# Second attention: score units of two PSUM banks, with separate banks for plain and turned scores

## The chip, the cores and the metric

One of the eight cores of a Trainium2 chip runs the program. A core has TensorE (PE: matrix products into PSUM, with PEld its weight loads), VectorE (DVE), ScalarE (ACT), GpSimd (POOL) and SyncE (SP, which issues the DMAs); each has its own queue, worked in order, and they meet at semaphores only. PSUM has 8 banks of 128 x 512 float32, and every matmul writes into one of them. The metric is the device time of one execution in microseconds, the median of several runs.

## The reference, cut to what matters

Six layers with residuals run over 8 sequences of 256 tokens with 128 channels: a mixture of experts, a linear attention with four blocks, the first mixture again, a mixture with expert choice (top-k), a causal attention with 16 heads of width 8, and the expert-choice mixture again. The change is in the causal attention:

```python
qkv = x @ W_attn + b_attn                 # x: layer-normed, [8, 256, 128]
q, k = rope(q), rope(k)                   # angles by head index; 16 heads, width 8
att = einsum('bhqd,bhkd->bhqk', q, k) / sqrt(8)
att = softmax(where(causal, att, -inf), axis=-1)
y = einsum('bhqk,bhkd->bhqd', att, v)
return y @ W_proj + b_proj
```

## The kernel before, in words

All semaphores and the order on every engine are written out by hand. The stage `attn1` has a function on each engine. A block `tb` is 512 tokens, two sequences. Per block, `project_in` (PE, 8 projections of 3 matmuls each) makes rotated queries and keys, which ScalarE (`hm`, L1475) and VectorE (`stk`, L2026) add and split into the stacked operand `stk`; `hm` has two buffers, so it may run at most two ahead of `stk`. In `stk` a head has 32 rows, so that a score product uses 32 of PE's 128 rows; four heads `g` with the same head group `hg` lie in the four row groups.

Each sequence's scores are computed twice. The **plain** scores (queries by keys, L955, with the causal mask added by further matmuls, L964 and L969) serve only for the row maximum, which VectorE takes from PSUM (L2034). The negated maxima are turned by PE (`maxima`), copied by ScalarE to `mT` (L1480), and put by a DMA into spare rows of `stk` (semaphore `m_placed`). The **turned** scores (keys by queries, L955 too) then come out with the maximum already subtracted; ScalarE takes the exponential from PSUM (`exps`, L1485), POOL zeroes the upper triangle (L2212), and PE multiplies by the values with a column of ones (`outputs`, L997 and L1000). ScalarE copies that to `ot` (L1490), PE flips it (L1008), VectorE divides (`normalise`, L2007 and L2010). Per block the result is turned (`turn`), split (yoT high on ScalarE, `low` on VectorE), projected (`project_out`) and added to the residual (`add`, L2019). The values of a block go through `values` (PE), vT (ScalarE), `values_turned` (PE) and a copy into `vaug` (VectorE).

Plain and turned scores of a sequence each have three units: `k` = 0 is the first half of the plain queries (16 products of 128 columns; for turned, `k` = 2), the others are 8 products of 256 columns, two head groups each. A unit fills four banks, one for each `g`, and one maximum or one exponential reads all four (128x2048). Banks 0 to 3 hold plain 0, plain 2, turned 0 and turned 1 in turn; banks 4 to 7 hold plain 1 and turned 2, and 4 and 5 also the outputs, 6 and 7 the flip, the values, the turning and the projections.

The loop (L1035) has ten passes, s = -1 to 8. A pass takes the plain scores of sequence s+1, the turned scores of s and the outputs of s-1, and its order on PE is: turned 0, plain 1, plain 0, (values or two projections), outputs of two head groups, plain 2, (two projections), the other outputs, turned 1, maxima, flip, turned 2, (four projections). "First" passes (s even) stack the next block if there is one, half of it between the maxima and half at the end of the pass; "second" passes (s odd) take the next block's values and the last block's output projection. With s = 7 the first parts of the following layer's norm and of its router start (`ln_centre`, `ln_variance` L573, `scores` L589), which lead to the top-k on VectorE.

Of the kernel before, what the change touches and what calls it, by code (L numbers as in the profile page):

```python
# [14 lines left out]
P = 128  # L15
# [17 lines left out]
HG = 4  # L33
# [103 lines left out]
def macaron(nc, a, const, out):  # L137
# [3 lines left out]
    with es:  # L141
# [169 lines left out]
        EARLY_BANK, LATE_BANK = {LN_FFN1: 4, LN_FFN1B: 6}, 2  # L311
# [25 lines left out]
        OUT_BANK, TURN_BANK = 7, (7, 7, 7, 6)  # L337
        V_BANK = 6

        def stack_bank(tb, k):  # L340

            if tb == 0:
                return k
            if tb == 1:
                return (4 if k < HG else 6) + k % 2
            return 6 + k % 2 if k < HG else k - HG

        def stack_mid(tb):

            return HG if tb == 1 else 0  # L350
# [179 lines left out]
        def _(pe):  # L530
# [405 lines left out]
            def attn1():  # L936
# [22 lines left out]
                def plain(s, k):  # L959

                    if k == 0:
                        products(0, s, 0, 1, 0, 0, P, range(HG), False)
                        for g in range(4):
                            ins = pe.matmul(ps[:, g, :], ident_b[:], cmask[:], start=False, stop=True, skip_group_check=True)  # L964
                    else:
                        bank = 4 if k == 1 else 0
                        products(bank, s, 0, 1, P, 0, SEQ, (2 * k - 2, 2 * k - 1), False)
                        for g in range(4):
# [4 lines left out]
                def turned(s, k):  # L973

                    if k < 2:
                        ins = products(0, s, 1, 0, 0, 0, SEQ, (2 * k, 2 * k + 1), True)
                    else:
                        ins = products(4, s, 1, 0, P, P, P, range(HG), True)
                    ins.then_inc(t_ready, 1)

                def maxima(s):
                    pe.wait_ge(mneg_done, s + 1)
                    for q in range(2):
                        ins = pe.transpose(ps[0:2 * HEADS, 6, q * P:(q + 1) * P],
# [41 lines left out]
                def project_out(tb):  # L1026
                    pe.wait_ge(yol_done, tb + 1)
                    mm3(pe, ps[:, OUT_BANK, :], wvp_hi[:, 1, :], wvp_lo[:, 1, :], yoT_hi[:], yoT_lo[:]).then_inc(proj_ready, 1)
# [6 lines left out]
                for s in range(-1, SEQS + 1):  # L1035
# [3 lines left out]
                    if 0 <= s < SEQS:  # L1039
                        if second and more and tb > 0:  # L1040
                            pe.wait_ge(stk_done, (tb + 2) * 2 * HG)
                        elif s > 0:
                            pe.wait_ge(exp_done, 3 * s - 1)
                        pe.wait_ge(m_placed, (s + 1) * (16 * 2))
                        turned(s, 0)
                    if s + 1 < SEQS:
                        pe.wait_ge(stk_done, ((s + 1) // SPB + 1) * (2 * HG))
                        if s >= 1:
                            pe.wait_ge(exp_done, 3 * s)
                        if s == 0:  # L1050
                            pe.wait_ge(stk_done, 2 * HG + HG)
                        plain(s + 1, 1)
                        if s >= 0:
                            pe.wait_ge(exp_done, 3 * s + 1)
                        plain(s + 1, 0)
                    if s + 1 < SEQS:
                        pe.wait_ge(max_done, 3 * (s + 1) + 1)
                    else:
                        pe.wait_ge(exp_done, 3 * min(s, SEQS))
                    if second and more:  # L1060
                        values(tb + 1)
                    if second and tb >= 1:
                        turn(tb - 1)
                    if s == SEQS - 1:
                        pe.wait_ge(exp_done, 3 * s + 1)
                        ln_centre(LN_FFN1B, 0)
                        ln_centre(LN_FFN1B, 1)
                    if first and more:
                        project_in(tb + 1, range(stack_mid(tb + 1), stack_mid(tb + 1) + 2))
                    if s >= 1:  # L1070
                        pe.wait_ge(vaug_done, (s - 1) // SPB + 1)
                        pe.wait_ge(causal_done, 3 * s)
                        outputs(s - 1, (0, 1))
                    if s + 1 < SEQS:
                        pe.wait_ge(max_done, 3 * (s + 1) + 2)
                        plain(s + 1, 2)
                    if second and more:
                        values_turned(tb + 1)
                    if s < 0:
                        project_in(1, range(2))  # L1080
                    if s == SEQS - 1:
                        ln_variance(LN_FFN1B, 0)
                        ln_variance(LN_FFN1B, 1)
                    if second and tb >= 1:
                        project_out(tb - 1)
                    if s == SEQS - 1:
                        scores(LN_FFN1B, 0)
                        scores(LN_FFN1B, 1)
                    if first and more:
# [1190 lines left out]
```

## Time and profile before

| | |
|---|---|
| median of 3 runs | 1083.9 us (1082.54 to 1086.08) |
| the profiled execution | 1078.49 us; its span 1076.8 us |
| busy | PE 933.8 (87%), PEld 628.2 (58%), DVE 708.1 (66%), ACT 619.6 (58%), POOL 337.8 (31%) |
| granted TensorE clock, mean | 0.925 of full speed |
| the stage that the change touches | 794.5 to 962.1 us |

Times are microseconds from the span's start unless marked ns. A busy time is a sum over a stretch; the window shows how much of it there could have been. The granted clock has two levels, 2.4 and 1.2 GHz, shown as 1 and 0.5, and a window shows its mean. A group names its line, engine, operation, what is written from what, and the shapes.

### The profile page before, as it was taken

To read this page: it belongs to the slowest core of one execution; us is meant where nothing else is said; L and a number is where in the kernel's file an instruction comes from. 1 tells how busy PE (TensorE), PEld (TensorE's weight loads), DVE (VectorE), ACT (ScalarE), POOL (GpSimd) and SP (SyncE) were. 2 spreads that over 40 slices of the span, in tenths; PEclk is the share of its full clock that TensorE was granted. 3 is DMA by queue.
4 is the path that set the end of the run, shared out by engine and by line. 5 is a ranking of instruction groups with operands and counts; after the bars stand their busy time and mean duration, and the time that the engine had idled before them with its cause. 6 is when DMAs were issued, how large, how long until landed. Compare 5 with 4: busy or idle time off the path is not lost.

```text
span 1076.8 us, 13026 instructions
## 1 busy us (share of the span) xinstructions
PE 933.8 (87%) x4507; PEld 628.2 (58%) x4507; DVE 708.1 (66%) x1413; ACT 619.6 (58%) x1003; POOL 337.8 (31%) x249
## 2 busy tenths in 40 slices
PE   6899999579999999879999997799967777777997
PEld 4678887123333333337788876488644545455886
DVE  3978887467778777646788886744276556547532
ACT  6555555268888888863555555544554545455454
POOL 1597777000000000001677775201201221123200
PEclk8999999689999999997999998699988778888999
DMA  5125110000000000003311110200000000001001
GB/s 172 43 79 159 66 62 27 0 1 0 1 1 1 0 1 0 1 0 118 76 64 64 64 50 16 63 21 2 1 0 3 4 2 2 4 1 39 1 2 40
DMA packets 30743, 33.64 MB, mean 31 GB/s; under 512 B 2062, under 2 KB 19798, under 8 KB 30678
## 3 DMA queue, kind: packets, MB, share of 16 engines
q1 hardware_dynamic: 30678, 32.81, 9.9%
q8 instruction: 36, 0.59, 0.2%
q14 instruction: 29, 0.24, 0.1%
HBM read 31.36 MB, written 1.18 MB: 30 GB/s over the span
## 4 chain that ended last, share of the span: by engine, by line
PE 61%; DVE 19%; ACT 11%; issue 4%; POOL 3%; DMA 0%; ACTq 0%; SPq 0%; DVEq 0%; POOLq 0%
PE ps L128 10%; PE ps L129 10%; PE ps L130 10%; PE ps L750 5%; PE ps L862 4%; PE ps L744 2%; ACT ex L1485 2%; PE ps L955 2%; PE ps L728 2%; ACT L1374 2%; POOL fl L2155 2%; DVE smax L2034 1%; PE ps L891 1%; PE ps L964 1%; PE ps L736 1%
## 5 line engine op out<-in xcount | busy, mean ns | idle before, releaser
L2155 POOL TENSOR_TENSOR fl<-fp,fh 128x512 fp32r<-128x512 f32 x144 | 223.5, 1568 | 126.3 <-ACT fh L1280 126.0
L1271 ACT ACTIVATE fs<-ps 128x512 f32<-128x512 f32 x144 | 86.2, 599 | 114.6 <-PE ps L130 114.4
L1743 DVE TENSOR_TENSOR fp<-fp,cwb 128x512 f32<-128x512 f32 x128 | 141.2, 1103 | 14.0 <-DVE fp L1736 0.9
L1736 DVE TENSOR_TENSOR fp<-fs,ps 128x512 f32<-128x512 f32 x144 | 98.2, 682 | 40.7 <-ACT fs L1271 40.1
L128 PE MATMUL ps<-z_hi,w_hi 128*128 128x512 f32 x288 | 117.0, 406 | 3.3 <-DVE fp L1736 3.3
L129 PE MATMUL ps<-z_lo,w_hi 128*128 128x512 f32 x288 | 116.6, 405 | 0.0
L130 PE MATMUL ps<-z_hi,w_lo 128*128 128x512 f32 x288 | 115.0, 399 | 0.0
L1280 ACT CAST fh<-fp 128x512 fp32r<-128x512 f32 x144 | 88.8, 617 | 36.8 <-DVE fp L1743 32.6
L2219 POOL TENSOR_TENSOR ln_sq<-ln_rs 128x512 f32<-128x512 f32 x20 | 21.1, 1056 | 272.4 <-ACT ln_rs L1337 272.4
L2212 POOL TENSOR_SCALAR_AFFINE_SELECT ex<-ex 128x1024 f32<-128x1024 f32 (+1 forms) x24 | 33.4, 1403 | 152.4 <-ACT ex L1485 152.4
L2034 DVE TENSOR_REDUCE smax<-ps 128x8 f32<-128x2048 f32 (+1 forms) x24 | 55.0, 2291 | 38.8 <-PE ps L969 31.9
L128 PEld LDWEIGHTS ps<-z_hi,w_hi 128*128 128x128 f32 x288 | 55.5, 193 | 19.7 <-DVE fp L1736 5.7
L862 PE MATMUL ps<-hid,w 128*128 128x256 f32 x256 | 66.7, 384 | 0.0
L744 PE MATMUL ps<-z,wb 128*128 128x512 f32 x128 | 62.3, 614 | 2.7 <-DVE qq L1840 2.7
L1421 ACT ACTIVATE hid<-ps 128x512 f32<-128x512 f32 x64 | 38.0, 598 | 45.3 <-PE ps L130 44.5
L130 PEld LDWEIGHTS ps<-z_hi,w_lo 128*128 128x128 f32 x288 | 55.9, 194 | 13.0
L129 PEld LDWEIGHTS ps<-z_lo,w_hi 128*128 128x128 f32 x288 | 55.3, 192 | 12.7 <-issue 0.2
L128 PE MATMUL ps<-fh,w_hi 128*128 128x512 f32 x144 | 57.4, 398 | 3.8 <-POOL fl L2155 3.8
L750 PE MATMUL ps<-hid,wb 128*128 128x512 f32 x128 | 60.1, 593 | 0.0
L736 PE MATMUL ps<-z,wb 128*128 128x512 f32 x96 | 49.1, 653 | 10.7 <-DVE z L1815 10.7
L732 PE MATMUL ps<-ln_sq,mean_w 128*128 128x512 f32 x72 | 40.5, 645 | 20.1 <-ACT ln_sq L1330 20.1
L129 PE MATMUL ps<-fl,w_hi 128*128 128x512 f32 x144 | 57.2, 397 | 0.0
(270 smaller groups left out, 2005.2 us busy)
## 6 DMA issues: line engine op xcount, KB each, us to landing
cwb<-cw_spread SPq DMA_DIRECT2D x64, 256.0 KB, 3.1
w_raw<-in_L_ffn_w_dram SPq DMA_DIRECT2D x20, 256.0 KB, 2.9
w_raw<-in_L_ffn_w_dram SPq DMA_DIRECT2D x4, 512.0 KB, 5.9
w<-in_L_ffn_w_dram SPq DMA_DIRECT2D x8, 256.0 KB, 4.4
x_tok<-in_L_attn_x_dram SPq DMA_DIRECT2D x4, 256.0 KB, 3.5
wb<-in_L_attn_W_dram SPq DMA_DIRECT2D x1, 1024.0 KB, 7.0
wb<-in_L_attn_W_dram SPq DMA_DIRECT2D x4, 256.0 KB, 4.0
out_dram<-z SPq DMA_DIRECT2D x4, 256.0 KB, 3.0
```

What stands on the lines that cost most here:

```text
L128: pe.matmul(out, w_hi, x_hi, start=start, stop=False)
L129: pe.matmul(out, w_hi, x_lo, start=False, stop=False)
L130: return pe.matmul(out, w_lo, x_hi, start=False, stop=stop)
L744: pe.matmul(ps[:, bank, :], wb[:, b, (4 + k) * P:(5 + k) * P], blk(z, t), start=True, stop=True).then_inc(a0_matmul[t], 1)
L750: pe.matmul(ps[:, A0_WO, :], wb[:, b, w], hid[:, k, :], start=(k == 0), stop=(k == FT - 1)).then_inc(a0_matmul[t], 1)
L862: ins = pe.matmul(ps[:, OUT1[n % 2], 0:SEQ], w2[:, e, ft * P:(ft + 1) * P], hid[:, g % RING1, f * SEQ:(f + 1) * SEQ], start=(ft == 0), sto ...
L1271: act.activation(fs[:, n % 2, :], ps[:, n % 2, :], ACT.Silu).then_inc(silu_done, 1)
L1280: act.copy(fh[:, n % RING0, :], fp[:, n % RING0, :]).then_inc(fhi_done, 1)
L1736: dve.tensor_tensor(f, fs[:, n % 2, :], ps[:, 2 + n % 2, :], ALU.mult).then_inc(prod_done, 1)
L1743: dve.tensor_tensor(f, f, cwb[:, x % CW_RING, :], ALU.mult).then_inc(weighed, 1)
L2034: dve.tensor_reduce(smax[:, s % 2, int(k > 0), :, hgs], ps[:, bank:bank + 4, :].rearrange("p g (h t) -> p g h t", h=HG if k == 0 else 2), ...
L2155: pool.tensor_tensor(fl[:, n % RING0, :], fp[:, n % RING0, :], f32(fh[:, n % RING0, :]), ALU.subtract).then_inc(flo_done, 1)
```

## The change

Each unit becomes two halves `j` = 0, 1 of two banks, for the heads `g` = 2j and 2j+1. The plain halves take banks 0,1 and 2,3 alternately, the turned halves 6,7 and 4,5. There are six maxima and six exponentials of 128x1024 per sequence in place of three of 128x2048, and the semaphores count sixths. The turned units come in the order 2, 0, 1. The outputs keep banks 4 and 5, the flip 6 and 7; maxima go to bank 0, values to 2, turning and projecting out to 1 or 3 (6 and 7 for the last block). Stacking uses banks 1, 2, 3, 0 (4 to 7 for the first half of block 1), and all its projections stand at the end of the pass on PE, ScalarE and VectorE. The order on PE within a pass is new, and so are the orders on ScalarE, VectorE and POOL around it.

```diff
-        OUT_BANK, TURN_BANK = 7, (7, 7, 7, 6)
-        V_BANK = 6
+        PLAIN = ((1, 0), (1, 1), (0, 0), (0, 1), (2, 0), (2, 1))
+        PLAIN_BANK = (0, 2, 0, 2, 0, 2)
+        TURNED = ((2, 0), (2, 1), (0, 0), (0, 1), (1, 0), (1, 1))
+        TURNED_BANK = (6, 6, 4, 4, 6, 4)
+        TURN_BANK, OUT_BANK = (1, 1, 3, 6), (1, 1, 3, 7)
+        M_BANK, V_BANK = 0, 2
...
-                def products(out, s, a_, b_, lo_a, lo_b, width, hgs, stop):
+                def products(out, s, a_, b_, lo_a, lo_b, width, hgs, j, stop):
                     for k, hg in enumerate(hgs):
-                        for g in range(4):
-                            ins = pe.matmul(ps[:, out + g, k * width:(k + 1) * width], part(s, a_, g, hg, lo_a, P),
+                        for g in (2 * j, 2 * j + 1):
+                            ins = pe.matmul(ps[:, out + g % 2, k * width:(k + 1) * width], part(s, a_, g, hg, lo_a, P),
                                             part(s, b_, g, hg, lo_b, width), start=True, stop=stop, skip_group_check=True)
                     return ins
...
+                def turned(s, i):
+
+                    k, j = TURNED[i]
+                    if i == 0:
+                        pe.wait_ge(m_placed, (s + 1) * (16 * 2))
+                        if s > 0:
+                            pe.wait_ge(exp_done, 6 * s - 1)
+                        else:
+                            pe.wait_ge(stk_done, 2 * HG + HG)
+                    elif i == 2:
+                        if s > 0:
+                            pe.wait_ge(ot_done, s)
+                    elif i == 4:
+                        if s > 0:
+                            pe.wait_ge(yo_done, s)
+                        else:
+                            pe.wait_ge(exp_done, 2)
+                    else:
+                        pe.wait_ge(exp_done, 6 * s + (1, 3, 4)[i // 2])
                     if k < 2:
...
+                        ins = products(TURNED_BANK[i], s, 1, 0, 0, 0, SEQ, (2 * k, 2 * k + 1), j, True)
                     else:
...
+                        ins = products(TURNED_BANK[i], s, 1, 0, P, P, P, range(HG), j, True)
                     ins.then_inc(t_ready, 1)
...
                 def flip(s):
                     pe.wait_ge(ot_done, s + 1)
+                    pe.wait_ge(exp_done, 6 * s + 8 if s + 1 < SEQS else 6 * s + 5)
...
+                    scored, soft, summed = s + 1 < SEQS, 0 <= s < SEQS, s >= 1
+                    if scored:
                         pe.wait_ge(stk_done, ((s + 1) // SPB + 1) * (2 * HG))
...
+                        if s >= 0:
+                            pe.wait_ge(mT_done, s + 1)
+                        if first and tb >= 2:
+                            pe.wait_ge(ln_in, u0 + NTB + tb - 1)
+                        plain(s + 1, 0)
+                        if first:
+                            pe.wait_ge(vaug_done, tb + 1)
                         plain(s + 1, 1)
...
                     if s == SEQS - 1:
...
+                        pe.wait_ge(mT_done, SEQS)
                         ln_centre(LN_FFN1B, 0)
                         ln_centre(LN_FFN1B, 1)
...
+                    if soft:
+                        turned(s, 0)
+                    if summed:
+                        pe.wait_ge(exp_done, 6 * s)
                         pe.wait_ge(vaug_done, (s - 1) // SPB + 1)
+                        pe.wait_ge(causal_done, 3 * s - 1)
+                        outputs(s - 1, (0, 1))
+                    if scored:
+                        plain(s + 1, 2)
+                    if soft:
+                        turned(s, 1)
+                    if scored:
+                        plain(s + 1, 3)
+                    if summed:
                         pe.wait_ge(causal_done, 3 * s)
...
+                        outputs(s - 1, (2, 3)).then_inc(o_ready, 1)
+                    if scored:
+                        plain(s + 1, 4)
+                    if soft:
+                        turned(s, 2)
+                    if scored:
+                        plain(s + 1, 5)
+                    if summed:
+                        flip(s - 1)
+                    if s == SEQS - 1:
+                        ln_variance(LN_FFN1B, 0)
+                        ln_variance(LN_FFN1B, 1)
+                        scores(LN_FFN1B, 0)
+                        scores(LN_FFN1B, 1)
+                    if soft:
+                        turned(s, 3)
+                    if second and tb >= 1:
+                        pe.wait_ge(max_done, 6 * min(s + 1, SEQS - 1) + 5)
+                        turn(tb - 1)
+                    if scored:
+                        maxima(s + 1)
+                    if second and more:
+                        pe.wait_ge(max_done, 6 * (s + 1) + 6)
+                        values(tb + 1)
+                    if soft:
+                        turned(s, 4)
+                    if second and tb >= 1:
+                        project_out(tb - 1)
+                    if soft:
+                        turned(s, 5)
                     if second and more:
                         values_turned(tb + 1)
                     if s < 0:
...
+                        project_in(1, range(HG))
+                    if first and more:
+                        ks = range(HG, 2 * HG) if tb == 0 else range(2 * HG)
+                        for k in ks:
+                            if k - ks[0] == 3:
+                                pe.wait_ge(mT_done, s + 2)
+                            if k - ks[0] >= 4:
+                                pe.wait_ge(stk_done, (tb + 1) * 2 * HG + k - 3)
+                            elif k == ks[0]:
+                                pe.wait_ge(max_done, 6 * (s + 1) + 6)
+                            project_in(tb + 1, (k,))
                     if s == SEQS - 1:
...
+                def exps(s, i):
+                    act.wait_ge(t_ready, 6 * s + i + 1)
+                    n, j = TURNED[i]
+                    bank = TURNED_BANK[i]
+                    act.activation(ex[:, s % 2, n, 2 * j:2 * j + 2, :].rearrange("p g t -> p (g t)"),
+                                   ps[:, bank:bank + 2, :].rearrange("p g t -> p (g t)"), ACT.Exp, scale=SCALE).then_inc(exp_done, 1)
...
+                    soft = 0 <= s < SEQS
+                    if soft:
                         exps(s, 0)
...
                     if s == SEQS - 1:
                         ln_square(LN_FFN1B, 0)
                         ln_copy(LN_FFN1B, 0)
+                    if soft:
+                        exps(s, 1)
+                    if s == SEQS - 1:
                         ln_square(LN_FFN1B, 1)
                         ln_copy(LN_FFN1B, 1)
...
                     if s >= 1:
                         stacked(s - 1)
+                    if soft:
+                        exps(s, 2)
+                        exps(s, 3)
+                    if second and tb >= 1:
+                        turn(tb - 1)
                     if s + 1 < SEQS:
                         maxima(s + 1)
+                    if second and more:
+                        values(tb + 1)
+                    if s == SEQS - 1:
+                        chances(1, 0)
+                    if soft:
+                        exps(s, 4)
+                        exps(s, 5)
                     if s < 0:
...
+                        stack(1, range(HG))
+                    if first and more:
+                        stack(tb + 1, range(HG, 2 * HG) if tb == 0 else range(2 * HG))
                     if s == SEQS - 1:
...
+                        for i in range(6):
+                            maximum(s + 1, i)
                         maxima(s + 1)
...
+                    if s >= 1:
+                        normalise(s - 1)
                     if s == SEQS - 1:
                         dve.wait_ge(sc_ready, part1(1, 0) + 1)
                         ln_root(LN_FFN1B, 0, SPB - 1)
                         part_weights(1, LN_FFN1B, 0)
...
+                    if second and tb >= 1:
+                        low(tb - 1)
+                        add(tb - 1)
+                    if second and more:
+                        values(tb + 1)
+                    if s < 0:
+                        stack(1, range(HG))
+                    if first and more:
+                        stack(tb + 1, range(HG, 2 * HG) if tb == 0 else range(2 * HG))
                     if s == SEQS - 1:
...
+                    for i, n in enumerate((2, 0, 1)):
+                        pool.wait_ge(exp_done, 6 * s + 2 * i + 2)
```

## Rows read from the trace of the kernel before

**Rows 1.** the page's part 4, the chain that ended last, by engine

```profile
PE 61%; DVE 19%; ACT 11%; issue 4%; POOL 3%; DMA 0%; ACTq 0%; SPq 0%; DVEq 0%; POOLq 0%
```

**Rows 2.** windows, one per pass: length, busy PE, PEld, DVE, ACT, POOL, clock

```profile
794.50:824.54 30.04, 19.72 (x163) 12.16 (x164) 20.58 (x21) 12.88 (x15) 2.27 (x3) 0.92 0.01 3
824.54:841.80 17.26, 12.99 (x158) 8.55 (x159) 8.71 (x9) 7.48 (x7) 4.17 (x4) 0.80 0.01 3
841.80:865.20 23.40, 19.98 (x166) 13.49 (x166) 13.76 (x16) 12.61 (x13) 6.09 (x4) 0.75 0.01 3
865.20:885.03 19.83, 14.92 (x172) 10.04 (x173) 10.07 (x11) 8.31 (x8) 2.27 (x3) 0.81 0.01 3
885.03:907.19 22.16, 17.59 (x166) 11.84 (x166) 13.68 (x16) 12.47 (x13) 6.10 (x4) 0.86 0.01 2
907.19:926.56 19.37, 14.64 (x173) 9.89 (x173) 10.07 (x11) 8.32 (x8) 2.28 (x3) 0.82 0.01 3
926.56:962.11 35.55, 27.79 (x299) 18.08 (x299) 13.57 (x31) 15.26 (x15) 8.24 (x6) 0.81 0.01 2
```

**Rows 3.** waits of PE in the stage: who for whom, total, times, longest

```profile
PE ps L955 <- ACT ex L1485: 9.2, 8, 1.8
```

**Rows 4.** groups by form in the stage: count, busy us, mean ns, idle before

```profile
L1485 ACT ACTIVATE ex<-ps 128x2048 f32<-128x2048 f32 x24 | 44.3, 1871 | 12.2 <-PE ps L955 12.2
L2034 DVE TENSOR_REDUCE smax<-ps 128x8 f32<-128x2048 f32 x16 | 36.7, 2291 | 31.9 <-PE ps L969 31.9
...
L2026 DVE SCALAR_TENSOR_TENSOR stk<-ps,bst,hm 128x512 fp32r<-128x512 f32 x25 | 18.2, 747 | 10.0 <-ACT hm L1475 10.0
L1475 ACT ACTIVATE hm<-ps,bstm,rope 128x512 fp32r<-128x512 f32 x24 | 17.9, 777 | 23.2 <-PE ps L130 22.9 <-DVE stk L2026 0.2
L2212 POOL TENSOR_SCALAR_AFFINE_SELECT ex<-ex 128x1024 f32<-128x1024 f32 x16 | 17.6, 1098 | 137.6 <-ACT ex L1485 137.6
...
L1490 ACT COPY ot<-ps 128x1024 f32<-128x1024 f32 x7 | 7.1, 1013 | 29.0 <-PE ps L1000 29.0
...
L1628 DVE TENSOR_REDUCE scm<-sce 128x8 f32<-128x64 f32 x1 | 0.2, 220 | 0.0
```

**Rows 5.** timeline at 2.4 GHz, one plain score unit: start, us, engine, line

```profile
874.79 0.39 PE L955 MATMUL ps<-stk 32*128 32x256 f32 x4
...
875.01 0.29 PE L955 MATMUL ps<-stk 32*128 32x256 f32 x4
...
875.23 0.61 PE L969 MATMUL ps<-cmask,ident_b 128*128 128x256 bf16 x4
...
875.88 2.29 DVE L2034 TENSOR_REDUCE smax<-ps 128x8 f32<-128x2048 f32 x1 [1.76 <-PE ps L969]
```

**Rows 6.** timeline of PE at 2.4 GHz: outputs, turned scores, projections

```profile
895.57 0.66 PE L997 MATMUL ps<-ex,vaug 128*32 128x256 f32 x8
...
897.04 0.51 PE L955 MATMUL ps<-stk 32*128 32x256 f32 x8
...
900.76 0.67 PE L955 MATMUL ps<-stk 32*128 32x128 f32 x16 [0.91 <-DVE yo L2010]
901.36 0.50 PE L128 MATMUL ps<-z_hi,wst_hi 128*128 128x512 f32 x1
...
902.86 0.40 PE L128 MATMUL ps<-z_hi,wst_hi 128*128 128x512 f32 x1
```

**Rows 7.** timeline of PE at 1.2 GHz, plain score units

```profile
885.03 0.80 PE L955 MATMUL ps<-stk 32*128 32x256 f32 x8 [1.76 <-ACT ex L1485]
885.77 1.03 PE L969 MATMUL ps<-cmask,ident_b 128*128 128x256 bf16 x4
886.73 1.12 PE L955 MATMUL ps<-stk 32*128 32x128 f32 x16
```

**Rows 8.** chain that ended last, in order of time, last pass

```profile
950.54 1.88 PE ps L573 x16
...
953.22 1.70 PE ps L589 x16
```

More of the change, by code:

```diff
@@ L1079, in attn1 @@
                     if s < 0:
-                        project_in(1, range(2))
-                    if s == SEQS - 1:
[L1082 to L1089, printed above, removed]
-                        pe.wait_ge(stk_done, (tb + 1) * 2 * HG + stack_mid(tb + 1) + 2)
-                        project_in(tb + 1, range(stack_mid(tb + 1) + 2, stack_mid(tb + 1) + 4))
@@ L1092, in attn1 @@
-                    if s >= 1:
-                        outputs(s - 1, (2, 3)).then_inc(o_ready, 1)
-                    if 0 <= s < SEQS:
-                        if s + 1 < SEQS:
-                            pe.wait_ge(max_done, 3 * (s + 1) + 3)
-                        else:
-                            pe.wait_ge(exp_done, 3 * s + 1)
-                        turned(s, 1)
-                    if second and more:
-                        pe.wait_ge(vaug_done, tb + 2)
-                    if first and more:
-                        pe.wait_ge(stk_done, (tb + 1) * 2 * HG + stack_mid(tb + 1) + 3)
@@ L1104, in attn1 @@
-                    if s + 1 < SEQS:
-                        maxima(s + 1)
-                    if s < 0:
-                        for k in range(2, 4):
-                            pe.wait_ge(stk_done, 2 * HG + k - 1)
-                            project_in(1, (k,))
-                    if second and tb >= 1:
-                        pe.wait_ge(ln_in, u0 + NTB + tb)
-                    if first and more:
-                        pe.wait_ge(stk_done, (tb + 1) * 2 * HG + stack_mid(tb + 1) + 4)
@@ L1126, in attn1 @@
-                    if first and more and tb > 0:
-                        pe.wait_ge(exp_done, 3 * s + 2)
-                        project_in(tb + 1, range(4, 8))
-                    if s == SEQS - 1:
-                        pe.wait_ge(exp_done, 3 * s + 2)
+                        project_in(1, range(HG))
[9 more added lines that the diff above has]
+                            project_in(tb + 1, (k,))
@@ L2059, in attn1 @@
                     if s + 1 < SEQS:
-                        maximum(s + 1, 1, 0)
-                        maximum(s + 1, 0, 1)
-                    if second and tb >= 1:
-                        low(tb - 1)
-                    if first and more:
-                        stack(tb + 1, range(stack_mid(tb + 1), stack_mid(tb + 1) + 2))
-                    if s + 1 < SEQS:
-                        maximum(s + 1, 2, 2)
-                    if second and more:
-                        values(tb + 1)
-                    if first and more:
-                        stack(tb + 1, range(stack_mid(tb + 1) + 2, stack_mid(tb + 1) + 3))
-                    if s + 1 < SEQS:
-                        maxima(s + 1)
-                    if second and tb >= 1:
-                        add(tb - 1)
-                    if first and more:
-                        stack(tb + 1, range(stack_mid(tb + 1) + 3, stack_mid(tb + 1) + 4))
-                    if s < 0:
-                        stack(1, range(4))
+                        for i in range(6):
+                            maximum(s + 1, i)
+                        maxima(s + 1)
+                    if s >= 1:
+                        normalise(s - 1)
                     if s == SEQS - 1:
@@ L2083, in attn1 @@
                         part_weights(1, LN_FFN1B, 0)
-                    if s >= 1:
-                        normalise(s - 1)
-                    if first and more and tb > 0:
-                        stack(tb + 1, range(4, 8))
+                    if second and tb >= 1:
[7 more added lines that the diff above has]
+                        stack(tb + 1, range(HG, 2 * HG) if tb == 0 else range(2 * HG))
                     if s == SEQS - 1:
```

118 lines of the change are left out of this document (25 added, 93 removed).

## The prediction

> **What bounds the kernel now.** I read the page first: the chain that ended last is mostly TensorE's, and VectorE and ScalarE hold about a third of it [rows 1]. The change touches one stage only, the second attention, so I cut the trace at the start of the first score product of each pass (794.5) and at the start of the top-k that follows (962.1) [rows 2]. The reader should see three things there. The stage is 167.6 us long. In no pass is an engine full: the pass from 865.20 takes 19.83 us with 14.92 of PE, 10.07 of VectorE and 8.31 of ScalarE; the pass from 885.03, which also stacks queries and keys for the next 512 tokens, takes 22.16 with 17.59, 13.68 and 12.47. And PE ran at a mean granted clock of 0.75 to 0.92; since it has only the levels 2.4 and 1.2 GHz, a mean c stands for a low share of 2(1-c): 4.8, 6.9, 11.7, 7.5, 6.2, 7.0 and 13.5 us, together 57.6 of the 167.6. So the stage is bound by hand-overs: scores and turned scores use the same four banks in turn, and PE's products wait longest for the exponentials that empty them [rows 3].
>
> The profiled execution took 1078.49 us (span 1076.8); the median of the timed runs is 1083.9, 5.4 above it. I work out a difference and add it to the median.
>
> **What the change costs per operation.** The halves split each 4-bank instruction of the readers. A maximum over 2048 columns takes 2.291 us and a reduction over 64 takes 0.220 [rows 4], so 1.04 ns a column: 1024 columns take 1.22. Bounds: 1.15 (half) to 2.29. Six instead of three cost VectorE 7.32 in place of 6.87 a pass. An exponential of 2048 takes 1.871 and a copy of 1024 from PSUM 1.013 [rows 4]; I take 1.02 (bounds 0.94 and 1.87), 6.1 in place of 5.6. Both engines have 5 us and more to spare in each pass [rows 2], so these 1.0 us matter only where they lie in a chain, and there they stand in the schedule below.
>
> PE is the part to look at. A score product uses 32 of the 128 rows, one row group per head g. In the trace four products, one for each g, start together at 874.79, the next four at 875.01, and the masks at 875.23 [rows 5]: a wave of four costs 0.22, whatever stands in it. The new halves put two g in a wave. Eight products (two waves of four) become two units of two waves of two: each unit costs 0.44 again, not 0.22. Sixteen 128-column products take 0.60 (900.76 to 901.36 [rows 6]), and half of them, again four waves, as much. Per pass the products so go from 2 x (0.44 + 0.44 + 0.60) = 2.96 to 5.92 us: **PE gets 3.0 us more to do in each of eight passes**. The 12 masks stay 12: four of 256 columns take 0.96 at 1.2 GHz (885.77 to 886.73 [rows 7]), so two take 0.22 to 0.24 at 2.4, and two of 512 columns twice that; I take 0.21 and 0.43. Bounds for a half unit: 0.22 (half a unit) to 0.44; I take 0.44, because four products that start together are busy for 0.39 in all [rows 5], so that nothing in a wave waits for its neighbour. At 1.2 GHz eight products take 0.74 (885.03 to 885.77 [rows 7]).
>
> Thus at 2.4 GHz a plain half costs 0.65 (0.44 + 0.21) or 1.03 (0.60 + 0.43), a turned half 0.44 or 0.60, the outputs of two head groups 1.47 (895.57 to 897.04), one projection 0.75 at most (two from 901.36 to 902.86), taken as 0.70 since the first of the two follows a change of shape [rows 6]. VectorE begins 0.65 after the four masks do (875.23 to 875.88 [rows 5]), of which 0.43 is the masks' own time: 0.22 from PE to a reader; I take 0.1 back to PE.
>
> **One pass written out** (second of a pair, full clock, 0 = first plain half). PE: plain 0 to 0.65, plain 1 to 1.30, turned 0 to 1.90, outputs to 3.38, plain 2 to 4.41, turned 1 to 5.01, plain 3 to 6.04, outputs to 7.52, plain 4 to 8.17. Turned 2 needs the bank that the copy ot reads (7.74 to 8.75): 8.87 to 9.31. Plain 5 to 9.96, flip to 10.87, turned 3 to 11.31. VectorE's maxima start at 0.87, 2.1, 4.63, 6.26, 8.39 and 10.18, so four of six wait for PE, which has 6.5 us of turned halves and outputs between them. The last ends at 11.4, the negated maxima at 12.0, normalise at 12.9. ScalarE: exponentials 2.1, 5.2, 9.5 and 11.5 to 12.55, then yoT to 13.16. VectorE's low half 13.9, project_out 14.0 to 14.7, add to 15.65; the next pass's first plain half waits for that add: **15.7**, against 19.83 and 19.37 before [rows 2]. Without add and project_out (pass from 824.54) 14.6 against 17.26. PE takes its queue in order, so of the waits that the change adds only turned 2's for ot costs (0.7): plain 5 stands behind it, and the last maximum behind that. Turned 4's wait for normalise holds back only turned 5 and the projections, and the outputs' for POOL's causal masks nothing: a mask takes 1.1 us [rows 4] and has the whole first half of the next pass.
>
> A first pass begins 0.2 later by the copy of the values; turned 4 and 5 run once normalise is done (13.1), their exponentials end at 15.85. Only behind these stand, on ScalarE, the eight hm of the next block, and each stk on VectorE lets the next but one hm begin: 0.777 + 0.747 alternating over two buffers [rows 4], one per 0.82, so the last stk ends at 15.85 + 7 x 0.82 + 0.78 + 0.78 = **23.2**. The next pass's first plain half waits for all eight. Before, four of the eight were hidden between the maxima: 23.40 and 22.16. Here is where the gain goes: PE's 8 x 0.70 fit under it.
>
> The opening (indices -1 and 0): six maxima end 9.2 after 794.5 and the row maxima are turned at 805.3, but the first turned half now waits until four stk of block 1 have left banks 6 and 7 (811.9), and four more stk follow the last exponential (823.3): 827.4, 33 against 30.04. The end: index 6 stacks nothing (14.2), index 7 has two centred norms, four halves with two squares and copies between, then variance 1.88 and scores 1.70 [rows 8], root, low, add and chances: 20.8, together 35.0 against 35.55.
>
> **Sum.** At full clock throughout: 33.0 + 14.6 + 23.2 + 15.7 + 23.2 + 15.7 + 35.0 = 160.4 against 167.6: **-7.2**. But 167.6 includes 57.6 us at 1.2 GHz, and 160.4 none. In a dense first ten microseconds of each pass PE is now the bound, so a low microsecond there does half the work and costs 0.5; I estimate that 0.8 of the low time meets such work. The order leaves PE idle for about 2.5 us at each stacking end (its last projection starts four stk before the last), and less elsewhere, so I take half the low time of before, 28 us: +11. **In all +4.** If none: -7. If all 57.6: +23 - 7 = +16.
>
> **Rivals.** (1) *The clock stays up*, since PE has 3 us more to do per pass and shorter waits: 0 to 6 us low, -7 to -4, so about 1078. For it: in the passes with the most stacking around (0.92 in the first of rows 2) the clock was best; against: 0.75 in the pass from 841.80, which stacks too. (2) *The stacking end at the low clock.* If PE falls while it waits for normalise (10.9 to 13.1), the eight projections cost 1.4 each at half speed, 11.2 from 14.2 on, in place of hm's pace of 0.82: the last stk ends near 27 in place of 23.2. Two such passes and the opening: +10 on top, 1098. It decides if the low stretch reaches past the third projection. (3) *Half waves are cheaper than whole ones.* If a wave of two took 0.11, PE would get nothing more to do; with the middle of the bounds, 0.165, it is spared 1.5 of the 3.0 in each pass, of which I put 1.3 in the chain: seven passes, -9 on the forecast, 1079. Against it speaks that the four of a wave start at one time and last no longer for being four [rows 5]. The Trainium skill, "TensorE: Matmul & The Clock Gate", section "Part 3: Packing small matmuls", gives 3.07 times the speed for four row tiles, not 4; an estimate by that page is that with two tiles a product costs 3.07/2 = 1.5 times as much, not 2 times, and the time would be this rival's. No row of this trace shows two tiles at a time. (4) *The change does nothing to the order*: PE takes its queue in order, so a turned half that waits for ot still holds up the next plain half, and each pass keeps its length: 1084.
>
> **How the numbers follow.** About 0.3% (3.3 us) is what a measurement of this kernel tells from none. The forecast, +4 with a spread of -2 to +10, has 0.42: 1088, own range 1082 to 1094. Clock up 0.25, low stacking end 0.20, cheap half waves 0.08, no effect 0.05. Faster (below 1080.6): 0.20 of the 0.25, the 0.08 and 0.04 of the forecast's lower end, 0.32. Same: 0.05 + 0.05 + 0.14 = 0.24. Slower: 0.24 + 0.20 = 0.44. The range goes to 1073 below (clock up with some of rival 3) and 1101 above (rival 2).
>
> **What would show it.** In the profile after: the products in waves of two, about 0.44 from a half's first product to its masks; 48 maxima near 1.22 and 48 exponentials near 1.02; passes alternating near 16 to 18 and 23 to 26; the eight hm in one run behind the last exponential with ScalarE at 0.82 each; the stage's mean clock near 0.9. Wrong: a wave of two at 0.11; first passes below 21, which would mean stacking overlaps with scores after all; second passes not below 19; or a change outside 794 to 980, where the code is the same.

## The result, and the profile after

The timed runs give 1093.5 us (median, 1092.0 to 1094.2) against 1083.7: ratio 1.0086, 95% interval 1.0065 to 1.0106, **9.8 us slower**. The profiled executions stand 13.5 us apart (1092.02 and 1078.49), the one of before 5.2 below its median, the one of after 1.4 below. Of the 13.5 the stage holds 9.6 (796.44 to 973.64 against 794.50 to 962.11); the top-k behind it takes 3.4 more, at a low clock; the stage begins 1.9 later, and 1.4 comes back at the end, both in code that is the same. In the fourteen profiles of this document the stage begins between 794.5 and 798.9, and what follows it takes 112 to 118 us. So a few microseconds outside the stage, which the prediction named as a sign of being wrong, are not shown to come from the change.

The page's part 4 answers to [rows 1]: more of the chain is PE's.

```profile
PE 65%; DVE 18%; ACT 10%; POOL 3%; issue 3%; DMA 0%; ACTq 0%; SPq 0%; DVEq 0%; POOLq 0%
```

The windows of the seven passes answer to [rows 2], same columns.

```profile
796.44:833.79 37.35, 30.82 (x156) 18.95 (x156) 22.08 (x27) 13.48 (x17) 4.22 (x3) 0.63 0.01 2
833.79:854.46 20.67, 20.35 (x157) 12.60 (x157) 8.51 (x11) 6.57 (x8) 3.12 (x2) 0.59 0.00 1
854.46:876.71 22.25, 17.99 (x176) 11.78 (x176) 14.88 (x20) 14.28 (x18) 5.32 (x4) 1.00 0.02 5
876.71:896.35 19.64, 19.27 (x164) 11.88 (x164) 9.80 (x13) 7.91 (x10) 3.12 (x2) 0.74 0.01 3
896.35:918.60 22.25, 18.03 (x177) 11.79 (x176) 14.87 (x20) 13.64 (x17) 5.32 (x4) 1.00 0.01 2
918.60:935.48 16.88, 16.27 (x164) 10.36 (x164) 9.95 (x13) 7.91 (x10) 3.12 (x2) 0.90 0.02 4
935.48:973.64 38.16, 33.11 (x312) 24.24 (x315) 15.18 (x34) 18.98 (x27) 9.56 (x7) 0.79 0.01 2
```

The two stacking passes, at full clock throughout, take 22.25 us. The passes behind a stacking end should be alike and are not: 20.67, 19.64 and 16.88 at clocks of 0.59, 0.74 and 0.90. By 2(1-c) times the length the stage has 27.6, 16.9, 0, 10.2, 0, 3.4 and 16.0 us at 1.2 GHz, **74.2 in all, against 57.6 before**.

Groups by form, answering to [rows 4], and PE's longest waits, answering to [rows 3]: the readers cost what halves should, and the longest wait is no longer for exponentials but for the last stk.

```profile
L1490 ACT ACTIVATE ex<-ps 128x1024 f32<-128x1024 f32 x48 | 48.6, 1022 | 60.8 <-PE ps L955 60.7
...
L2043 DVE TENSOR_REDUCE smax<-ps 128x8 f32<-128x1024 f32 x16 | 19.6, 1225 | 22.8 <-PE ps L968 22.8
L1479 ACT ACTIVATE hm<-ps,bstm,rope 128x512 fp32r<-128x512 f32 x24 | 17.7, 777 | 5.6 <-PE ps L130 5.2 <-DVE stk L2034 0.4
...
L2034 DVE SCALAR_TENSOR_TENSOR stk<-ps,bst,hm 128x512 fp32r<-128x512 f32 x24 | 17.3, 751 | 15.4 <-ACT hm L1479 15.4
```

```profile
PE ps L955 <- DVE stk L2034: 8.7, 5, 2.3
PE ps L1004 <- DVE mneg L2055: 5.4, 6, 2.0
PE ps L955 <- ACT ot L1495: 3.1, 5, 1.5
```

PE's products at 2.4 GHz (timeline: start, us), answering to [rows 5]. Four products, a half unit, stand 0.42 ahead of their masks, where before eight stood 0.44 ahead. Two masks hold PE for 0.32 (855.75 to 856.07), where the prediction counted 0.21. The eight at 867.07, though, are turned halves 4 and 5 together: the projection behind them starts after 0.44, since neighbours with complementary head groups fill each other's waves.

```profile
854.47 0.50 PE L955 MATMUL ps<-stk 32*128 32x256 f32 x4
...
854.89 0.39 PE L972 MATMUL ps<-cmask,ident_b 128*128 128x256 bf16 x2
...
855.75 0.39 PE L972 MATMUL ps<-cmask,ident_b 128*128 128x256 bf16 x2
...
856.07 0.66 PE L955 MATMUL ps<-stk 32*128 32x128 f32 x8
...
867.07 0.52 PE L955 MATMUL ps<-stk 32*128 32x256 f32 x8 [0.33 <-DVE yo L2018]
867.51 0.50 PE L128 MATMUL ps<-z_hi,wst_hi 128*128 128x512 f32 x1
```

The stacking end in the timeline: hm in pairs, 0.83 each (869.43 to 874.42 is six), the last stk, and then the wait of the next pass.

```profile
869.43 1.45 ACT L1479 ACTIVATE hm<-ps,bstm,rope 128x512 fp32r<-128x512 f32 x2
...
874.42 1.45 ACT L1479 ACTIVATE hm<-ps,bstm,rope 128x512 fp32r<-128x512 f32 x2 [0.21 <-PE ps L130]
875.23 1.42 DVE L2034 SCALAR_TENSOR_TENSOR stk<-ps,bst,hm 128x512 fp32r<-128x512 f32 x2 [0.23 <-ACT hm L1479]
...
876.71 0.50 PE L955 MATMUL ps<-stk 32*128 32x256 f32 x4 [2.34 <-DVE stk L2034]
```

The stacking end of the opening, by contrast, meets the low clock (one window, then ScalarE): hm waits for projections at 1.2 GHz, and the next one starts 1.28 later in place of 0.83.

```profile
828.00:831.00 3.00, 3.00 (x9) 2.32 (x8) 1.00 (x2) 2.46 (x4) 1.10 (x1) 0.50 0.02 8
...
829.94 0.78 ACT L1479 ACTIVATE hm<-ps,bstm,rope 128x512 fp32r<-128x512 f32 x1 [0.26 <-PE ps L130]
...
831.22 0.78 ACT L1479 ACTIVATE hm<-ps,bstm,rope 128x512 fp32r<-128x512 f32 x1 [0.50 <-PE ps L130]
```

What follows the wait at 876.71 (windows, columns as above): PE starts at full clock, falls to 1.2 GHz near 880, and stays there to about 889 although it is busy all the time.

```profile
876.71:880.00 3.29, 3.29 (x42) 2.19 (x46) 2.35 (x2) 1.02 (x1) 0.00 (x0) 0.91 0.00 0
880.00:883.00 3.00, 3.00 (x26) 1.53 (x18) 0.00 (x0) 0.00 (x0) 0.00 (x0) 0.50 0.00 0
...
886.00:889.00 3.00, 3.00 (x34) 1.74 (x36) 1.23 (x1) 0.19 (x1) 1.30 (x1) 0.50 0.02 5
889.00:892.00 3.00, 3.00 (x29) 1.95 (x27) 2.09 (x2) 1.84 (x2) 0.00 (x0) 0.89 0.00 0
```

In the last pass variance and scores, 1.88 and 1.70 us in [rows 8], meet the low clock too (chain in order of time).

```profile
957.88 3.06 PE ps L573 x16
960.93 3.44 PE ps L589 x16
```

### The profile page after: what moved, and what is told of

The parts are those of the page before. It is cut to its first block, busy times and chain, and to the rows that moved or that the text cites. A ratio compares the mean times of both kernels' runs of the same rounds, so it can differ in the third digit from the quotient of the medians.

```text
span 1090.3 us, 13069 instructions
## 1 busy us (share of the span) xinstructions
PE 968.0 (89%) x4507; PEld 650.0 (60%) x4507; DVE 712.3 (65%) x1437; ACT 623.4 (57%) x1027; POOL 338.5 (31%) x249
## 4 chain that ended last, share of the span: by engine, by line
PE 65%; DVE 18%; ACT 10%; POOL 3%; issue 3%; DMA 0%; ACTq 0%; SPq 0%; DVEq 0%; POOLq 0%
PE ps L128 10%; PE ps L129 10%; PE ps L130 10%; PE ps L750 5%; PE ps L862 4%; PE ps L955 4%; PE ps L744 2%; PE ps L728 2%; ACT L1378 2%; PE ps L833 2%; PE ps L1017 2%; POOL fl L2154 2%; DVE smax L2043 1%; PE ps L891 1%; PE ps L736 1%
## 5 line engine op out<-in xcount | busy, mean ns | idle before, releaser
L1490 ACT ACTIVATE ex<-ps 128x1024 f32<-128x1024 f32 x48 | 48.6, 1022 | 60.8 <-PE ps L955 60.7
L2043 DVE TENSOR_REDUCE smax<-ps 128x4 f32<-128x1024 f32 (+1 forms) x48 | 57.9, 1223 | 36.7 <-PE ps L968 22.8
L955 PE MATMUL ps<-stk 32*128 32x128 f32 (+1 forms) x512 | 54.2, 345 | 13.9 <-DVE stk L2034 8.7
L744 PE MATMUL ps<-z,wb 128*128 128x512 f32 x128 | 62.4, 614 | 2.7 <-DVE qq L1848 2.7
L955 PEld LDWEIGHTS ps<-stk 32*128 32x128 f32 x512 | 38.5, 218 | 39.7 <-issue 13.6
```

What stands on the lines that cost most here:

```text
L744: pe.matmul(ps[:, bank, :], wb[:, b, (4 + k) * P:(5 + k) * P], blk(z, t), start=True, stop=True).then_inc(a0_matmul[t], 1)
L955: ins = pe.matmul(ps[:, out + g % 2, k * width:(k + 1) * width], part(s, a_, g, hg, lo_a, P), part(s, b_, g, hg, lo_b, width), start=True, ...
```

## The experiments

Three theories: **1**, half-filled waves put PE's extra work on the path; **2**, the granted clock decides; **3**, the stacking behind the last exponentials holds up the next pass. Every kernel ran beside the kernel before on its own chip, and ratios are to that one. "Low" is the stage's time at 1.2 GHz, as above.

**halves_before**: the half units alone, in the old order.

```
-    for g in range(4): ...products..., masks
+    for gs in ((0, 1), (2, 3)):
+        for g in gs: ...products..., masks
```

> The kernel before, with one part of the change alone: each score unit's products are issued for two head groups, then for the other two (plain units with their masks between), in the same banks, with the same readers and semaphores. Theory 1 (half-filled waves put 3.0 us of PE work into each pass, and it lies on the path): PE's busy time in 794 to 962 rises by about 20 us, passes grow by 1 to 2 us each, 1089 to 1099. Theory 2 (the granted clock decides; PE's extra work by itself does not): within 3 us of the kernel before, 1081 to 1087. Theory 3 (the stacking moved behind the last exponentials decides): no difference that comes from stacking, 1084 to 1087.

Measured: 1104.1 us, ratio 1.0185 (1.0158 to 1.0213), above even theory 1's range. PE is busy 31.6 us longer in the stage (159.2 against 127.6). But the low time rose too, from 58 to 102 us, so this run alone doesn't part theories 1 and 2.

**fill_after**: idle PE is kept busy. The fillers behind a stacking end wait for the last exponential, which frees their bank; nothing else differs.

```
+    def fill(bank, n):
+        for k in range(n):
+            pe.matmul(ps[:, bank, :], ident_b[:], cmask[:], start=True, stop=True)
+    fill(7, 6)   # ahead of maxima(0)
+    pe.wait_ge(exp_done, 6 * s + 6)
+    fill(7, 8)   # behind the last project_in of a stacking pass
+    fill(3, 6)   # ahead of turned(7, 2)
```

> The kernel after, with idle PE given products whose result nobody reads (identity by the mask, 512 columns, 0.21 us each at 2.4 GHz): 6 ahead of the first turned maxima, 8 behind the last projection of each stacking pass, 6 ahead of the third turned half of the last index. Nothing else differs. Theory 2: low time of the stage falls from 74 us to 45 or less, and with some 0.3 us per low microsecond the time falls by 5 to 10 us, 1084 to 1088. Theories 1 and 3: the fill lies in waits, so 0 to +2 us, 1093 to 1096.

Measured: 1075.6, ratio 0.9913 (0.9895 to 0.9932): **18 us under the kernel after**, beyond theory 2's range, and theories 1 and 3 failed. Its windows:

```profile
797.17:832.27 35.10, 31.30 (x167) 18.09 (x170) 22.11 (x27) 13.34 (x17) 4.22 (x3) 0.71 0.01 3
832.27:846.51 14.24, 12.69 (x156) 8.51 (x158) 8.51 (x11) 6.81 (x8) 3.12 (x2) 1.00 0.01 2
846.51:868.76 22.25, 19.53 (x181) 12.47 (x182) 14.89 (x20) 14.30 (x18) 5.32 (x4) 1.00 0.01 4
868.76:884.12 15.36, 14.60 (x163) 9.70 (x164) 9.95 (x13) 7.92 (x10) 3.12 (x2) 1.00 0.01 3
...
921.73:957.04 35.31, 30.66 (x316) 21.30 (x321) 15.33 (x34) 18.90 (x27) 9.54 (x7) 0.88 0.01 2
```

The three passes behind stacking ends fall from 20.67, 19.64 and 16.88 to 14.24, 15.36 and 15.34; the stacking passes keep 22.25. The stage takes 159.9 with 28.8 us low, so 45.4 low microseconds cost 17.3: 0.38 each, as an average over the stage.

**late45_after**: turned halves 4 and 5 behind the stacking.

```
-    turned(s, 4); turned(s, 5); project_in(...)    # ACT: exps 4, 5; stack
+    project_in(...); turned(s, 4); turned(s, 5)    # ACT: stack; exps 4, 5
```

> The kernel after, with turned halves 4 and 5 and their exponentials moved behind the stacking of the next block in the three passes that stack (PE: behind the projections; ScalarE: behind the eight hm). Theory 3 (the serial stacking end holds back the next pass): the passes of 22.25 us fall to about 20, three of them, so -5 to -6 us, 1088; the two exponentials of 1.02 us then run beside the next pass's first plain halves. Theory 1: PE has the same work, 0, 1093. Theory 2: 0 plus or minus 3 by whatever the clock does.

Measured: 1081.8, ratio 0.9974 (0.9951 to 0.9998), 11.6 under the kernel after. Theory 3's term is there: 22.25 fell to 20.29 and 20.31, both at clock 1.00, so 1.95 a pass. Of the rest, most came with the clock: the pass behind the opening took 15.79 at 0.89, not 20.67 at 0.59, and low time fell to 54 us, which no theory had foreseen.

```profile
832.81:848.60 15.79, 14.23 (x157) 9.18 (x159) 8.50 (x11) 7.81 (x10) 4.22 (x3) 0.89 0.01 2
848.60:868.89 20.29, 17.15 (x174) 11.89 (x174) 14.96 (x20) 13.38 (x18) 4.22 (x3) 1.00 0.01 4
```

**nomask_after** and **nomask_before**: no mask products, in either order.

```
-    products(..., stop=False); masks; ins.then_inc(s_ready, 1)
+    products(..., stop=True).then_inc(s_ready, 1)
```

> The kernel after without the twelve mask products of each index: the row maxima are taken over all keys, hidden ones too (the outputs still leave them out). It takes 4 x 0.21 + 2 x 2 x 0.43 = 2.6 us at 2.4 GHz out of PE's queue in each pass. Theory 1 (PE's queue is the bound of a pass's first ten microseconds): second passes fall by 1.5 to 2.5 us, first ones by 1, in all -8 to -13 us, 1081 to 1085. Theory 2: the less PE has to do the lower its clock, so most of it is given back, 1090 to 1094. Theory 3: only the passes without stacking gain, -4 us, 1089.

> The kernel before without the mask products: the row maxima are taken over all keys, the hidden ones too (the outputs leave them out as before). Control for nomask_after, which gained 31 us on the kernel after. Theory 1 (PE's own work is on the path only in the dense order of the change): -5 to -10 us here, 1074 to 1079, since PE waits for banks a quarter of the time. Theory 2 (with less PE work the clock falls): -3 to +3 us, 1081 to 1087. If the masks cost the same everywhere: -20 us or more, below 1064.

Measured: 1062.1, ratio 0.9798 (0.9772 to 0.9825), in the new order, 31 us less than the kernel after and below every range; 1074.9, ratio 0.9934 (0.9905 to 0.9962), in the old, as theory 1 had it, where PE waits for banks and the low time rose to 75 us. In the new order a stacking pass at full clock takes 2.57 us less, all of the 2.6 at which PE's masks were put; of the 31 us some 8 are clock, an estimate by 0.38 for each of the 20 low microseconds that are gone (54 left):

```profile
847.67:867.35 19.68, 14.97 (x163) 10.38 (x162) 14.68 (x20) 13.94 (x18) 5.31 (x4) 1.00 0.01 3
867.35:881.30 13.95, 12.77 (x152) 8.78 (x152) 9.85 (x13) 7.79 (x10) 3.11 (x2) 0.88 0.01 4
```

So theory 1 holds for where the path runs: in the new order PE's queue is the bound. In the old order the same products are worth 7 us by the ratio and 9 by the medians, so that PE is on the path there only in part.

**fill_before**: the control for the clock.

```
+    fill(0, 16)   # ahead of the first project_in
+    fill(0, 7)    # ahead of the first score product
+    fill(7, 6)    # ahead of maxima(0)
+    # behind a stacking end the fill has new waits, for the exponential
+    # that frees bank 0 and for stk
+    fill(0, 7)    # (8 behind a stacking end) ahead of turned(s, 0), s > 0
```

> The kernel before with idle PE given products that nobody reads (as in fill_after): 16 ahead of the first projection, 7 ahead of the first score product, 6 ahead of the first turned maxima, and 7 or 8 ahead of the first turned half of each index from 1 on, where PE waits 1.7 to 2.8 us. Nothing else differs. Theory 2 (the clock is what separates the two kernels): the stage's low time falls from 58 us to about 30 and the time by some 0.35 us for each, -10 us, 1074, level with the filled kernel after (1075.6), so that the change's order by itself is worth nothing. Theory 1 (in the kernel before PE is not the bound, so its clock matters less there): -3 us or less, 1081 to 1084, and the order of the change is worth the 6 to 8 us that its full-clock schedule promised, less half waves.

Measured: 1075.4, ratio 0.9932 (0.9900 to 0.9964): theory 2. The old order gains 8.1 us by its clock and is then level with the filled new one, whose ratio is 0.9913. At full clock it takes 21.0 and 16.4 us a pass, the new 22.25 and 15.35:

```profile
848.02:869.03 21.01, 17.45 (x183) 11.27 (x182) 13.58 (x16) 13.02 (x14) 6.22 (x4) 1.00 0.01 3
869.03:885.41 16.38, 13.21 (x171) 8.80 (x171) 9.97 (x11) 7.68 (x7) 2.20 (x2) 1.00 0.01 4
```

**halves_fill_before**: both edits in the old order.

> The kernel before with half units (as halves_before) and with idle PE filled (as fill_before). Half waves alone cost 20 us at an uneven clock, with 44 us more at the low level; here the clock is held up. Theory 1 (half waves are the cost at any clock): passes of 16.4 and 21.0 us rise by 1.2 to 2.0 us each, 1084 to 1090. Theory 2 (they cost by the clock that they bring down): 1075 to 1079, level with fill_before.

Measured: 1098.9, ratio 1.0134 (1.0076 to 1.0192), dearer than either theory. The stacking pass took 22.51 at 0.97, 1.5 more than with whole waves; the other 20.73 at 0.84, 4.4 more. The stage's low time is 58.0 against 13.9. Without fill it was 102.1 against 58.0. **Both pairs differ by 44 us**: half units cost PE time and, in the old order, bring the clock down, filled or not. Each low time is that of one profiled execution, so the equal 44 is chance, but the direction is not: the mean granted clock of the six executions is 0.920 to 0.932, that of the nine of fill_before 0.934 to 0.949.

```profile
858.12:880.63 22.51, 19.49 (x183) 12.51 (x182) 13.60 (x16) 12.65 (x13) 5.22 (x4) 0.97 0.01 3
880.63:901.36 20.73, 18.08 (x172) 11.26 (x173) 10.07 (x11) 7.77 (x7) 2.20 (x2) 0.84 0.01 3
```

**fours_fill_after**: waves of four again where banks allow.

```
-    TURNED = ((2, 0), (2, 1), ...
+    TURNED = ((2, 1), (2, 0), ...
-    plain(s + 1, 0); plain(s + 1, 1); ... turned(s, 4); turned(s, 5)
+    plain01(s + 1); ... turned45(s)     # all four g in one run, banks 0-3 and 6, 7, 4, 5
```

> The kernel fill_after with waves of four again where the banks allow it: plain halves 0 and 1 (banks 0 to 3) and turned halves 4 and 5 (banks 6, 7, 4, 5) are issued over all four head groups at once, and turned half 1 takes the row groups that plain half 3 behind it does not use. It takes about 0.44 + 0.44 + 0.6 of PE's 3.0 us per pass away again. Theory 1 (half waves are the cost at any clock): passes of 22.25 and 15.35 us fall by 0.6 to 1.2, in all -5 to -8 us, 1067 to 1071. Theory 2 alone (with the clock filled up nothing is left to gain): 1075 to 1077.

Measured: 1068.8, ratio 0.9860 (0.9825 to 0.9896), 6.8 under fill_after: theory 1. Passes at full clock fell from 22.25 to 21.23 and, by less than it said, from 15.35 to 14.96.

```profile
845.53:866.76 21.23, 18.72 (x182) 11.85 (x182) 14.09 (x19) 13.35 (x17) 5.31 (x4) 1.00 0.01 3
866.76:881.72 14.96, 13.30 (x164) 8.87 (x164) 10.47 (x14) 8.35 (x10) 3.52 (x3) 1.00 0.01 3
```

**fill2_after**: the opening and the end filled too.

```
+    fill(0, 16); fill(0, 7)   # opening, as in fill_before
+    fill(0, 8)    # ahead of the last index's project_out
+    fill(3, 12)   # ahead of turn(NTB - 1)
```

> The kernel fill_after with idle PE filled at the opening (16 ahead of the first projection, 7 ahead of the first score product) and at the end (8 ahead of the last index's output projection, 12 ahead of the last turn) too. It asks what the change's order takes with the clock up in the opening and the end, where fill_after still had 20.4 and 8.5 us low. If the schedule of the prediction holds there as it did in the five passes between (33.0 and 35.0 us at full clock): 35.1 and 35.3 stay as they are, 1074 to 1076. If a low microsecond costs 0.38 there as in the rest of the stage: the opening falls to 28 to 31, the end to 32 to 34, 1066 to 1071.

Measured: 1073.8, ratio 0.9891 (0.9849 to 0.9933), under the first range and over the second. The end fell to 33.50 us with 3.4 low, as a cost of 0.38 has it; the opening stayed at 35.15 with 20.4 low, so what its terms are at full clock stays unmeasured:

```profile
796.51:831.66 35.15, 31.73 (x170) 18.08 (x171) 22.13 (x27) 13.39 (x17) 4.21 (x3) 0.71 0.01 3
...
921.08:954.58 33.50, 31.77 (x326) 20.66 (x329) 15.31 (x34) 18.10 (x25) 8.88 (x7) 0.95 0.01 2
```

**Versions with several edits**, all faster than both kernels: best1 (nomask_after, late45_after and fill together), best2 (best1 with waves of four) and masked_best (waves of four, late45 and fill, masks kept).

> The kernel after with three edits together: no mask products (row maxima over all keys), turned halves 4 and 5 behind the stacking in the three stacking passes, and idle PE filled at the opening (16, 7 and 6), behind those turned halves (7), and in the last two indices (6, 8 and 12). If the edits add up (1062 without masks; -2 us for each of three stacking passes; the clock's share of the opening and the end): passes of 17.7 and 14 us, 1048 to 1054. If PE is no longer what binds once the masks are gone, the fill gives nothing and only the moved halves count: 1056. If late turned halves collide with the next pass: 1060.

> The kernel best1 (no masks, late turned halves 4 and 5, idle PE filled) with the waves of four of fours_fill_after, and 5 more fillers ahead of plain half 2 in the first two indices. If PE's products still bind without the masks: passes of 17.7 and 12.6 us fall by 0.3 to 0.8, 1040 to 1044. If VectorE's maxima (six of 1.22 us, then the negated maxima) bind now: no change, 1045 to 1048.

> The kernel after with the masks kept, and with waves of four where the banks allow them, late turned halves 4 and 5, and idle PE filled at the opening, the stacking ends and the end. If the gains add (fours_fill_after 1068.8, 2 us for each of three stacking passes, 3 to 6 us for the opening and the end): 1056 to 1062. If the moved halves only take what the waves of four had won: 1066 to 1069.

Measured: best1 **1046.7, ratio 0.9665** (0.9629 to 0.9701), a little under the range for gains that add; masked_best 1063.9, ratio 0.9812 (0.9769 to 0.9855), between its two ranges: against fours_fill_after its stacking passes fell from 21.23 to 19.28, but the others rose from 14.96 to 15.32; best2 1050.0, ratio 0.9689 (0.9645 to 0.9733), outside both of its ranges and no better than best1. Its stacking passes gained 0.5 us and the others lost 1.0, for a reason that wasn't followed up. The windows are best1's.

```profile
838.06:855.79 17.73, 15.89 (x170) 11.07 (x169) 14.84 (x20) 13.32 (x18) 4.22 (x3) 1.00 0.02 5
855.79:868.43 12.64, 11.31 (x152) 8.14 (x152) 9.85 (x13) 8.73 (x12) 4.22 (x3) 1.00 0.01 4
```

## Why the prediction was right, and where its size was off

The forecast was +4 (1088) and the result +9.8, inside the range and on the side that had most of the chance. That the number came so near is partly luck: the schedule was too long, the clock's term too small, and the errors went opposite ways. By 0.38 for each, the 74.2 low microseconds of the kernel after stand for some 28 us, and a stage without them for some 149 (an estimate; fill2_after gives the same), where 11 and 160.4 were put. And signs that the prediction named came out against it: of the three second passes, 20.67 and 19.64 are not below 19, and the stage's mean clock was 0.79, not near 0.9.

The account that the runs give for the stage:

| | old order | new order |
|---|---|---|
| as it ran (low time) | 167.6 (58) | 177.2 (74) |
| with PE filled (low time) | 157.6 (13.9) | 158.1 (23.7, fill2_after) |
| what the fill took away | 10.0 | 19.1 |

With idle PE filled the change is worth +0.5 us, and the ratios of the two filled kernels (0.9891 and 0.9932) can't be told apart; the other 9.1 of the 9.6 went with the low time that the fill took away. Filled is not full clock: the new order kept 9.8 low microseconds more, 8.5 of them in the opening, so what the change is worth at full clock throughout is not shown. In passes where both orders ran at 1.00, the new one takes 1.2 more with stacking and 1.0 less without.

- **Half waves at 0.44**: right (0.42). A half whose neighbour uses the other two head groups costs nothing more, though (eight products in 0.44), so a stacking pass pays some 0.4 to 0.9 less than the 3.0 counted. The Trainium skill, "TensorE: Matmul & The Clock Gate", section "Part 3: Packing small matmuls", gave the estimate beside rival 3 its 3.07, and that estimate of 1.5 times fails here: two waves of two took 0.42 and two of four 0.44, so a product in a wave of two costs 1.9 times as much. The span model of the same section, by which a pack lasts as long as one product and about 4 ns more for each further tile, agrees with these two numbers.
- **Masks at 0.21 and 0.43**: too cheap; 0.32 (855.75) and 0.53 (858.73 to the next product at 859.26).
- **Readers at 1.22 and 1.02, hm at 0.82**: right (1.22, 1.02, 0.83).
- **Pass lengths at full clock**: 14.6, 23.2, 15.7, 23.2 and 15.7 were forecast, 14.24, 22.25, 15.36, 22.27 and 15.34 measured (fill_after): 92.4 against 89.5.
- **The -7.2**: mis-sized. It set a schedule at full clock against a stage with 57.6 low microseconds in it, as if these cost the old order nothing. The 43.7 of them that the fill took away cost it 10 us (fill_before), 0.23 each.
- **The clock's +11**: the step that failed in size. "I take half the low time of before, 28 us" became 74; the price, 0.40, was right (0.38). The stacking end's idle was named as the place, and the fill there shows it for the passes behind; that the clock then falls in busy work and stays low for most of a pass was not foreseen. The opening and the end were forecast as 33.0 and 35.0 at full clock and took 35.15 and 33.50 with 23.7 us still low, so those terms were too long, by an amount that no run shows. This hid part of the clock's error.
- **Rivals**: (1) the clock did not stay up. (2) Two stacking ends ran at full clock (22.25 at 1.00); the one in the opening met the low clock, and its four hm started over 3.27 us (828.90 to 832.17) in place of 2.5, so it cost some 0.8, where the rival had +10 for all three. (3) is refuted by the 0.42 and by fours_fill_after, where waves of four gave 6.8 us back, (4) by the filled passes at 1.00 (15.35 against 16.38, 22.25 against 21.01). With the last two turned halves ahead of it, the stacking end costs 1.95 us a pass (late45_after); masked_best shows 0.36 of that given back in the next pass.

What stays open: why the clock falls in the opening even when filled, and why half units bring 44 us of low time in the old order.

One remedy was not tried, four head groups in the two banks of a half: the Trainium skill, "TensorEngine Tiling (Array Packing)", section "Restrictions and Gotchas", says that different row tiles cannot access one PSUM bank at the same time. No run here shows it.

## What to carry to other kernels

Splitting a unit by head groups to free banks halves the fill of PE's row groups, and each product then costs nearly twice as much (four in 0.42 us, where eight took 0.44); pair halves that use different row groups, or split only where PE waits. Before reading the gain of an order, compare it with idle PE filled in both versions: here 79 products in idle time took 19 us off the stage in the new order, and a like fill 10 in the old. Once PE is the bound, look at what it does that the result doesn't need: leaving the masks out saved 7 to 9 us in the old order and 31 in the new. A row maximum over hidden keys serves as long as no hidden score lies so far above the visible ones that all their exponentials underflow; no run here tests such data.

## What was not expected of the hardware

With eight fillers of 0.21 us in a wait of 2.3, the pass behind it ran at clock 1.00 throughout; without them three like passes of one execution had 16.9, 10.2 and 3.4 us low. In the second of them PE shows no idle time from 876.71 to 892, and its clock was 0.50 from 880 to 889 all the same.
